# A ring of four for the state-times-q products, decay values written in place, per-tile scatter waits and an f32 quarters' table

## What is computed

```python
# block 0: gated linear attention (4 heads, chunks of 64), then a small per-unit FFN
x = x + ga * gla(ln(x) * (1 + ca) + sa)
x = x + gb * ffn0(ln(x) * (1 + cb) + sb)
# block 1: convolution, then this recurrence over the tokens for 512 channels x 16 states
dtv = sigmoid(dt_t + dt_head_b)
dtv = dtv / (1.0 + dtv * sum(k_t * k_t))
state = state * (1.0 - dtv[..., None] * (k_t * k_t)) + (x_t * dtv)[..., None] * k_t
y_t = einsum('bdn,bn->bd', state, q_t)
x = x + ga * ((y + D * x_in) * silu(z)) @ out_proj.T
# block 1's FFN: 8 experts; each expert takes the 512 tokens of a batch element
# with the highest probability (top_k), runs 256 -> 1024 (gelu) -> 256 on them,
# scales by the probability and adds the rows to the output
out = zeros.at[batch_idx, m].add(g * h)
```

## Time and profile before

| | us |
|---|---|
| median of 3 runs | 1870.5 (1869.12 to 1871.28) |
| the profiled execution | 1872.29 |
| its span, first to last instruction | 1870.5 |

### The profile page before, as it was taken

The page is one execution under the profiler, slowest core; times in us unless marked ns, Lnnn a source line. Parts: engine busy times, 40 slices in busy tenths (PEclk is TensorE's granted clock), DMA queues, the critical chain, the costliest instruction groups (busy, mean ns, idle before and its releaser), DMA issues.

```text
span 1870.5 us, 34289 instructions
## 1 busy us (share of the span) xinstructions
PE 1724.7 (92%) x12348; PEld 1486.4 (79%) x12348; DVE 1477.8 (79%) x3114; ACT 1379.2 (74%) x2705; POOL 1371.7 (73%) x644
## 2 busy tenths in 40 slices
PE   6688999999999999999999999998876999999997
PEld 5567788887878888797888879787665888899996
DVE  3557888888888888888888888888898678766663
ACT  3468878888888888888888888887742756666663
POOL 0008899898989989899998989999998333444442
PEclk9899999999999999999999999999897999999998
DMA  4013222222132322323232132223222444555551
GB/s 194 1 29 73 61 67 69 65 62 86 50 86 65 73 64 58 89 52 84 64 74 71 50 91 60 73 57 85 72 54 82 133 109 103 133 136 135 136 136 23
DMA packets 120888, 149.88 MB, mean 80 GB/s; under 512 B 8208, under 2 KB 111120, under 8 KB 120336
## 3 DMA queue, kind: packets, MB, share of 16 engines
q1 hardware_dynamic: 108432, 130.91, 25.4%
q0 software_dynamic: 12288, 16.79, 5.2%
HBM read 121.98 MB, written 17.30 MB: 74 GB/s over the span
## 4 chain that ended last, share of the span: by engine, by line
PE 76%; POOL 7%; DVE 6%; issue 6%; ACT 3%; DMA 0%; POOLq 0%; DVEq 0%; ACTq 0%
PE po L1819 9%; PE pY L1136 9%; PE pD L1119 9%; PE ph L1819 9%; PE pA L718 6%; POOL room L1177 3%; PE pA L620 3%; PE pB L915 3%; DVE room L1168 3%; PE pB L925 3%; POOL room L1187 3%; PE pB L1215 3%; PE pB L946 2%; PE pA L646 2%; PE pA L611 2%
## 5 line engine op out<-in xcount | busy, mean ns | idle before, releaser
L1187 POOL TENSOR_TENSOR room<-room 128x1024 f32<-128x1024 f32 x256 | 606.9, 2371 | 180.6 <-DVE room L1102 143.2
L1168 DVE TENSOR_TENSOR_SCAN room<-pD,last,room 128x256 f32<-128x256 f32 x1024 | 691.7, 732 | 50.4 <-PE pD L1119 38.8
L1177 POOL TENSOR_TENSOR room<-room 128x1024 f32<-128x1024 f32 x256 | 606.5, 2369 | 64.3 <-PE pY L1136 63.4
L1149 ACT ACTIVATE room<-room,fixed,kkT 128x512 f32<-128x512 f32 x512 | 406.3, 806 | 54.3 <-PE pD L1119 52.4
L1119 PE MATMUL pD<-fixed,room 128*128 128x128 f32 x2048 | 318.6, 279 | 47.2 <-DVE room L1168 45.1
L1136 PE MATMUL pY<-fixed,room 128*128 128x128 f32 x2048 | 319.2, 280 | 15.9 <-POOL room L1177 15.9
L1119 PEld LDWEIGHTS pD<-fixed,room 128*128 128x128 f32 x2048 | 244.1, 144 | 75.0 <-issue 41.4
L1136 PEld LDWEIGHTS pY<-fixed,room 128*128 128x128 f32 x2048 | 249.2, 145 | 65.8 <-POOL room L1177 30.0
L330 POOL DMA_INDIRECT xg<-xn_rows,W x64 | 69.4, 1084 | 199.2 <-DVE W L324 184.1
L1778 ACT ACTIVATE h<-ph 128x512 f32<-128x512 f32 x128 | 76.7, 599 | 136.6 <-PE ph L1819 94.7
L1819 PE MATMUL po<-w_up,h_up 128*128 128x256 f32 x512 | 148.9, 291 | 3.2 <-DVE h_rest L1686 2.6
(11 more groups left out here) (310 smaller groups left out, 3591.0 us busy)
## 6 DMA issues: line engine op xcount, KB each, us to landing
room<-kq_rows SPq DMA_DIRECT2D x256, 256.0 KB, 5.3
w_in<-w_d SPq DMA_DIRECT2D x32, 1024.0 KB
room<-ndS SPq DMA_DIRECT2D x16, 512.0 KB, 3.3
xt<-x_in SPq DMA_DIRECT2D x16, 256.0 KB, 3.0
y_out<-xo SPq DMA_DIRECT2D x16, 256.0 KB, 2.1
xn_rows<-xnC SPq DMA_DIRECT2D x16, 256.0 KB, 2.1
W<-weights SPq DMA_DIRECT2D x1, 1808.0 KB, 9.3
W<-weights SPq DMA_DIRECT2D x1, 1697.5 KB, 16.8
```

The lines of the kernel that those rows point to most:

```text
L1149: act.activation(decT[:, m % 2, t, :], turn2(ndT, it, NT * DI, t * DI, DI), ACT.Identity, bias=ones_s[:, 0:1], scale=turn2(kkT, it, NT * D ...
L1168: dve.tensor_tensor_scan(run, pD[h][:, k2 * TB:(k2 + 1) * TB], run, last[:, bass.ds(later(it) * (DS * DT) + m * DT + k, 1)], ALU.mult, ALU ...
L1177: pool.tensor_tensor(sq[:, m % 2], st[:, m % 4], kqb[:, m % SLOTS, 1, :].unsqueeze(1).broadcast_to([P, DT, TB]), ALU.mult).then_inc(sem("r ...
L1187: pool.tensor_tensor(st[:, m % 4], turn2(u, it, DT * TB).rearrange("p (k t) -> p k t", k=DT), kqb[:, m % SLOTS, 0, :].unsqueeze(1).broadca ...
```

## The change

- `sq` becomes a ring of four (`SQ`): the product of state m waits for the sum of state m-4 in place of m-2.
- `ndS` is gone: ACT and DVE compute the decay values in the half of `ndT` that belongs to the block, PE transposes from there, and ACT's first decay waits for DVE's `ndt`. The DMA copy, its semaphore, SP's wait for `ndt` and ACT's wait for the earlier copy are gone.
- `tmpT` becomes a view of the buffer of the turned keys (`kgt`).
- `quarter` is f32 in place of bf16 (both `entries` and `onehot` stay bf16).
- The scatter waits for `scaled` tile by tile.

```diff
+SQ = 4
...
-             ("lo", LT, F32), ("quarter", SL * LT // 2, BF16),
+             ("lo", LT, F32), ("quarter", SL * LT, F32),
...
-        ndS = sb("ndS", [P, NT, DI])
-
-        ROOM = [("st", 4 * DT * TB), ("sq", 2 * DT * TB), ("kqb", SLOTS * 2 * TB), ("decT", 2 * NT * DI), ("ndT", 2 * NT * DI),
+
+        ROOM = [("st", 4 * DT * TB), ("sq", SQ * DT * TB), ("kqb", SLOTS * 2 * TB), ("decT", 2 * NT * DI), ("ndT", 2 * NT * DI),
...
-        tmpT = sb("tmpT", [P, NT, DI])
+        tmpT = kgt[:, :, :, :].rearrange("p t h n -> p t (h n)")
...
+        def nd_of(it):
+            return turn2(ndT, it, NT * DI).rearrange("p (t d) -> p t d", t=NT)
...
-                act.wait_ge(sem("nd_in"), it * 16)
                 act.wait_ge(sem("ut_mm"), it * 2)
                 for t in range(NT):
-                    i = act.activation(ndS[:, t, :], pB[1 - t][:, :], ACT.Ln, bias=ones_s[:, 0:1], scale=ks[:, t:t + 1])
+                    i = act.activation(nd_of(it)[:, t, :], pB[1 - t][:, :], ACT.Ln, bias=ones_s[:, 0:1], scale=ks[:, t:t + 1])
...
-                    i = dve.tensor_tensor(ndS[:, t, :], pB[1 - t][:, :], ndS[:, t, :], ALU.mult)
+                    i = dve.tensor_tensor(nd_of(it)[:, t, :], pB[1 - t][:, :], nd_of(it)[:, t, :], ALU.mult)
...
-                        act.wait_ge(sem("nd_in"), it * 16 + 16)
+                        act.wait_ge(sem("ndt"), it + 1)
...
-                pool.wait_ge(sem("summed"), it * 2 * DS + 2 * m - 2)
-                pool.tensor_tensor(sq[:, m % 2], st[:, m % 4], kqb[:, m % SLOTS, 1, :].unsqueeze(1).broadcast_to([P, DT, TB]),
+                pool.wait_ge(sem("summed"), it * 2 * DS + 2 * (m - SQ + 1))
+                pool.tensor_tensor(sq[:, m % SQ], st[:, m % 4], kqb[:, m % SLOTS, 1, :].unsqueeze(1).broadcast_to([P, DT, TB]),
...
-                sp.wait_ge(sem("ndt"), f + 1)
                 sp.wait_ge(sem("kq_out"), f * 16 + 16)
-                sp.dma_start(turn2(ndT, f, NT * DI), flat(ndS[:, :, :])).then_inc(sem("nd_in"), 16)
...
             def scatter(k):
-                pool.wait_ge(sem("scaled"), (k + 1) * SL)
                 if k % E == 0:
                     pool.wait_ge(sem("x_out"), ((k // E + 1) * BPB + 1) * 16)
                 for s in range(SL):
+                    pool.wait_ge(sem("scaled"), k * SL + s + 1)
```

More of the change, by code:

```diff
@@ L77 @@
     halo=1, in_x=2, x_cp=6, tail=1, conv=(DCV - 1) * DT, xs=2, in_z=2, sz=2, dkq_mm=1, dkq=1, kq_out=16,
-    k_turn=1, kk=3, dt_mm=2, sig=2, den_ln=1, den=1, ndt=1, nd_in=16, ut_mm=2, u=2,
+    k_turn=1, kk=3, dt_mm=2, sig=2, den_ln=1, den=1, ndt=1, ut_mm=2, u=2,
     inp=DS, dec_t=2 * DS, dec_mm=2 * DS, scanned=DT * DS, saved=DS, read_out=DS, summed=2 * DS, opened=2,
@@ L475, in layers @@
         st = part(room_at, "st").rearrange("p (n k t) -> p n k t", n=4, k=DT)
-        sq = part(room_at, "sq").rearrange("p (n k t) -> p n k t", n=2, k=DT)
+        sq = part(room_at, "sq").rearrange("p (n k t) -> p n k t", n=SQ, k=DT)
         kqb = part(room_at, "kqb").rearrange("p (n w t) -> p n w t", n=SLOTS, w=2)
@@ L950, in front_pe @@
                 for kp in range(2):
-                    halves(pB[kp], kp, ndS).then_inc(sem("ut_mm"), 1)
+                    halves(pB[kp], kp, nd_of(it)).then_inc(sem("ut_mm"), 1)
         def front_act(act, it, n):
@@ L1033, in front_act @@
                 act.wait_ge(sem("kk"), it * 3 + 3)
-                act.wait_ge(sem("nd_in"), it * 16)
                 act.wait_ge(sem("ut_mm"), it * 2)
                 for t in range(NT):
-                    i = act.activation(ndS[:, t, :], pB[1 - t][:, :], ACT.Ln, bias=ones_s[:, 0:1], scale=ks[:, t:t + 1])
+                    i = act.activation(nd_of(it)[:, t, :], pB[1 - t][:, :], ACT.Ln, bias=ones_s[:, 0:1], scale=ks[:, t:t + 1])
                 i.then_inc(sem("den_ln"), 1)
                 act.wait_ge(sem("den_ln"), it + 1)
-                act.activation(ndS[:, :, :], ndS[:, :, :], ACT.Exp, scale=-1.0).then_inc(sem("den"), 1)
+                act.activation(nd_of(it), nd_of(it), ACT.Exp, scale=-1.0).then_inc(sem("den"), 1)
         def front_dve(dve, it, n, back):
@@ L1135, in scan_pe @@
                 for k in range(DT):
-                    i = pe.matmul(pY[:, t, k * P:(k + 1) * P], sq[:, m % 2, k, t * P:(t + 1) * P], ident_s[:, :],
+                    i = pe.matmul(pY[:, t, k * P:(k + 1) * P], sq[:, m % SQ, k, t * P:(t + 1) * P], ident_s[:, :],
                                   start=False, stop=(m == DS - 1), is_transpose=True, skip_group_check=True)
```

## The result

The changed kernel took 1864.74 us in the median of 13 runs (1861.93 to 1867.06), the kernel before 1870.52 beside it (13 runs, 1868.93 to 1872.77): ratio 0.997, 95% interval 0.9963 to 0.9978, so 5.8 us less. Run again at the end of the study it came to 1864.97 and 0.9972.

The account below looks back on a forecast made before the run. PE bounds the kernel where five stages overlap and in the expert lists, POOL in the last two blocks' scans. Savings of 1.1 + 5.6 = 6.7 us from the median 1870.5 give 1863.8 us; 8-in-10 range 1859 to 1866.5.

Parts of the forecast that it names:

- Scatter waits, minus 5.6: At the end, list 15's first three scatters go before the last tile is scaled, saving 3 x 1.86 = 5.6 us.
- Rival (d): At the end, queued transfers set the last landing, not the last issue; about 1869 us, chance 0.05.
- The ring, 0 in the middle: From 250 to 1240 us, the ring of four gains nothing: u pins POOL each turn and no matmul waits for it.
- Rival (b): The ring works in the middle turns too: 13 turns gain 1.6 us each, about 1842 us, chance 0.03.
- The ring, minus 1.1 in the last two blocks: In the last two blocks, POOL's 1.35 us wait for PE goes and its chain of products ends 1.1 us earlier.
- Decay values, 0: Decay values written in place remove sixteen 512 KB transfers from SP's queue; worth 0, between minus 1.9 and 0 us.
- The f32 table, 0: At list 0's start, the quarters' table in f32 gains 0: L302 is held because both inputs are in SBUF.
- Rival (a): The f32 table lifts the hold on L302; what follows moves up 4.1 us more, 1859.7 us, chance 0.10.
- Rival (c), the clock: TensorE's clock stays low through list 0 after the last blocks' pauses: 16.7 us slower, 1880.5 us, chance 0.03.

Follow-up runs that it names:

- the wait of two: The changed kernel with four buffers kept but the wait for the sum of state m-2 put back: 1866.78 us, ratio 0.9979 to before.
- the probe: The changed kernel with three unused 128-element DVE instructions ahead of list 0's first product, beside POOL's last three products; the f32 copy from SBUF took 4.10 us.
- the scatters undone: The changed kernel with the old single scatter wait for all four tiles put back: 1870.02 us, ratio 0.9996 to before.
- the kernel with the earlier rows: The PSUM kernel plus PE's last output projection ahead of the transposes of list 0's rows, and SP's first weight refill waiting for those rows: 1862.07 us, ratio 0.9959.
- the PSUM kernel: The changed kernel with list 0's quarters and places also written to PSUM and read from there by place(0): 1862.56 us, ratio 0.9957 to before.
- the last kernel: The kernel with the earlier rows, with the transposes of list 0's rows between the two halves of the last output projection: 1859.08 us, ratio 0.9944 to before.

## Why the prediction was right

The forecast was 1863.8 us, 6.7 less than before; it came to 1864.74, 5.8 less, in the range and by the mechanisms named. By its steps:

- **Scatter waits, minus 5.6.** Right in place and size. The last scatter starts 0.28 us behind the last scaled tile's instruction, and 3 x 1.86 us are gone: 5.41 between the profiles, 6.5 in the medians of the edit alone, with the forecast inside its interval. Rival (d), an end set by queued transfers, is refuted: 7.67 us from the last scatter's start to the end, where it had been 7.56.
- **The ring, 0 in the middle.** Right, and shown by the wait of two: POOL's 53 us came back and the turn stayed. Rival (b) falls, though the chain of waits leads through POOL in each turn: PE's 1.64 us ahead of L1121 are there in the profiles before and after and in that of the wait of two alike.
- **The ring, minus 1.1 in the last two blocks.** 1.0 measured inside seven profiles, four with the ring of four and three without. The profile after alone would have said 0.31, because its kq wait was 0.42 us longer and the rest is how a single execution falls; the two medians alone would have said 2.0. What I had as fact beside it, that POOL alone sets the pace from 1343 on, holds only behind the stretch around 1345: there DVE's scans are as late.
- **Decay values, 0** between minus 1.9 and 0: 1.0004 with an interval of 0.0009 to either side, so right as far as the times can tell. The bounds were not: "the edit can only remove one" left out that it could cost anything, and the profiles show two turns longer by 0.5 us together.
- **The f32 table, 0.** Right: the hold is 4.5 us with either type. The reason given was the inputs' place. It holds for two inputs in SBUF, but the probe shows a single-input copy held too, so the line I drew was too narrow. Rival (a) falls, and its price was too high as well: lifting the hold by PSUM brought 2.4 us, not 4.1. The rival counted the instructions behind L302 as moving freely, yet the comparison L306 is of the same kind and would have been held in its place, as the profile with the scatters undone shows, where the product was through early and the comparison took 4.43 us:

```profile
1433.92 4.43 DVE L307 TENSOR_TENSOR W<-W 128x2048 bf16<-128x2048 f32 x1
```

- **Rival (c), the clock.** It did not go slower: from 1460 to 1480 the granted clock is 1.00. But the clock has a part in front of that, which I had not priced. In 1440 to 1445 of the changed kernel, behind PE's 5.6 us of waiting for the comparison, it is 0.50 (1.2 GHz), as in the kernel before. In the kernel with the earlier rows it is 0.50 and 0.67 in the two halves of the projection, which is why that took 6.20 us where the PSUM kernel took 4.54 at 0.80: length times mean clock is about 3.6 us for both. In the last kernel, the projection's first eight matmuls took 3.78 us at 1.2 GHz and the other eight 1.89 us at 2.4 GHz, in its windows:

```profile
1441.60:1445.30 3.70, 3.70 (x9) 2.84 (x10) 0.00 (x0) 0.00 (x0) 0.00 (x0) 0.50 0.45 115
1446.70:1448.50 1.80, 1.80 (x9) 1.28 (x8) 0.25 (x1) 1.80 (x4) 0.00 (x0) 1.00 0.24 98
```

## What to carry to other kernels

When the last transfers of a kernel wait for one count that covers all of them, wait piece by piece: the price of the issues then lies under the work that makes the pieces, and here the end was the one place where it was paid in full. Removing a wait of a slack engine can bring nothing: look first for what pins that engine next (here u), and count the gain only in the stretch where nothing does. And when an instruction behind another engine's run takes ten times its usual time, look at where its tensors lie, and at the next instruction of the same kind, before its type.

## What the runs showed of the hardware

- The hold can last over a boundary between POOL's instructions. In nine of the profiles DVE's instruction came up during the second of POOL's last three products, which ran back to back, and was free only at the end of the third (4.10 to 4.59 us). In a tenth, with the scatters undone, it came up at the same place and got in between the second and the third, with no pause that the profile names: 2.28 us for DVE's product, and 7.20 for POOL's three in place of 6.96. What decides between the two is open.
- It goes both ways, with the first one served: 4.05 us for POOL's product behind DVE's comparison.
- POOL's issue of a gather takes 0.956 us in the median of 64, but some around the last scan take longer, with DVE at work on SBUF beside them: 2.73 for the first gather of the changed kernel, which ended about 1 us behind DVE's comparison, and 1.72 and 1.48 in the last kernel, beside its comparison and its subtractions. It isn't a rule: in both kernels a gather beside such a subtraction took 0.95 or 0.96.

```profile
1436.24 1.72 POOL L338 DMA_INDIRECT xg<-xn_rows,W  x1 [0.30 <-issue]
1438.27 1.48 POOL L338 DMA_INDIRECT xg<-xn_rows,W  x1 [0.31 <-issue]
1440.06 0.95 POOL L338 DMA_INDIRECT xg<-xn_rows,W  x1 [0.30 <-issue]
```

That DVE is the cause is not shown: it was not tried by itself.
